# Keys, values and queries of six groups from three fp32r products instead of plain fp32

## The reference

```
q   = layernorm(x) @ Wq.T ;  k, v = ctx @ Wkv.T            # 16 heads of 16, ctx is 192 wide
x   = x + tanh(g0) * softmax(mask(q k' / 4)) v
h   = layernorm(x)
moe = sum over the top 2 of 8 experts: score * (silu(p) * g) @ fc2[e],  p, g = split(h @ fc1[e])
x   = x + tanh(g1) * (moe + (silu(h @ gate_w) * (h @ up_w)) @ down_w)
```

## Time and profile before

| | |
|---|---|
| median of 3 runs | 344.87 us (344.2 to 347.57) |
| the profiled execution | 345.56 us |
| its span in the trace | 343.8 us |
| granted TensorE clock, mean | 0.975 of 2.4 GHz |
| the step loop | from about 22 us to about 155 us |
| PE, DVE, ACT, POOL busy | 90%, 74%, 50%, 35% of the span |

### The profile page before, as it was taken

One profiled execution on the slowest core, in us unless ns is written; L12 is line 12 of the kernel. 1 busy time (PEld: TensorE's weight loads), 2 busy tenths in 40 slices (PEclk: granted clock), 3 DMA queues, 4 the chain that ended last, 5 costly groups with the idle time before them and its releaser, 6 DMA issues.

```text
span 343.8 us, 8094 instructions
## 1 busy us (share of the span) xinstructions
PE 311.0 (90%) x2484; PEld 254.7 (74%) x2484; DVE 253.2 (74%) x780; ACT 170.7 (50%) x325; POOL 119.6 (35%) x133
## 2 busy tenths in 40 slices
PE   8858989989889886777989999999999999999986
PEld 7746767877768764664537488888888988888865
DVE  5566668899989897885889936676666667643795
ACT  2534767766667562555682326544444454424131
POOL 5731121217171715155440062943433433431000
PEclk9998999999999996969999999999999999999999
DMA  8886586666666565211134001333333333202951
GB/s 231 245 235 195 175 214 215 172 185 183 179 187 188 155 187 154 96 65 62 62 110 140 0 15 49 100 96 101 100 109 90 92 95 92 76 27 77 422 176 61
DMA packets 34917, 46.52 MB, mean 135 GB/s; under 512 B 5599, under 2 KB 29539, under 8 KB 34370
## 3 DMA queue, kind: packets, MB, share of 16 engines
q1 hardware_dynamic: 27714, 28.51, 28.9%
q10 hardware_dynamic: 3712, 8.98, 8.1%
q0 software_dynamic: 3456, 8.56, 7.2%
HBM read 21.55 MB, written 12.62 MB: 99 GB/s over the span
## 4 chain that ended last, share of the span: by engine, by line
PE 49%; DVE 19%; SPq 10%; DMA 9%; issue 7%; POOL 4%; ACT 2%; DVEq 0%; POOLq 0%
PE ps L1606 24%; SPq L354 5%; DMA stacks<-work 4%; SPq L361 4%; DVE mx L895 4%; PE ps L1283 3%; DVE x_all L1242 3%; PE ps L1656 2%; PE ps L1348 2%; PE ps L1578 2%; DMA expert_rows<-v_s,slot_u 2%; PE ps L1484 2%; PE ps L1598 2%; POOL dispatched L494 2%; PE ps L1381 2%
## 5 line engine op out<-in xcount | busy, mean ns | idle before, releaser
L539 POOL DMA_INDIRECT expert_rows<-v_s,slot_u x39 | 38.3, 981 | 62.5 <-ACT v_s L804 49.8
L895 DVE TENSOR_REDUCE mx<-ps 128x8 f32<-128x1024 f32 x32 | 39.1, 1223 | 11.5 <-PE ps L1348 10.8
L502 POOL TENSOR_TENSOR work<-work 128x512 bf16<-128x512 f32 x16 | 18.5, 1154 | 60.1 <-ACT work L590 60.0
L621 ACT ACTIVATE probs<-ps 128x1024 f32<-128x1024 f32 x32 | 32.6, 1019 | 11.6 <-PE ps L1381 10.1
L1192 DVE TENSOR_TENSOR act<-ps,sil 128x256 f32<-128x256 f32 x39 | 16.6, 425 | 29.2 <-ACT sil L797 29.1
L797 ACT ACTIVATE sil<-ps 128x256 f32<-128x256 f32 x39 | 15.0, 384 | 39.6 <-PE ps L1606 39.4
L1606 PE MATMUL ps<-fc_hi,xs_hi 128*128 x78 | 34.2, 438 | 0.0
L1606 PE MATMUL ps<-fc_lo,xs_hi 128*128 x78 | 30.9, 396 | 0.0
L1606 PE MATMUL ps<-fc_hi,xs_lo 128*128 x78 | 30.8, 395 | 0.0
L1348 PE MATMUL ps<-stacks 96*128 96x128 bf16 x256 | 20.6, 226 | 10.7 <-DVE mx L895 6.1
L804 ACT ACTIVATE v_s<-ps,wt 128x256 f32<-128x256 f32 x39 | 18.5, 474 | 19.6 <-PE ps L1606 19.6
(11 more groups left out here) (209 smaller groups left out, 808.7 us busy)
## 6 DMA issues: line engine op xcount, KB each, us to landing
stacks<-work SPq DMA_DIRECT2D x93, 128.0 KB, 2.8
xs_in<-dispatched SPq DMA_DIRECT2D x39, 129.0 KB, 2.1
fc_s<-in_fc ACTq DMA_DIRECT2D x8, 512.0 KB, 3.7
fc_s<-in_fc ACTq DMA_DIRECT2D x8, 256.0 KB, 4.3
stacks<-expert_rows SPq DMA_DIRECT2D x2, 1024.0 KB, 5.9
probs<-expert_rows SPq DMA_DIRECT2D x2, 1024.0 KB, 10.0
ctx_s<-in_ctx_t SPq DMA_DIRECT2D x8, 192.0 KB, 3.3
x_all<-in_x SPq DMA_DIRECT2D x1, 1536.0 KB, 7.9
```

The source lines that it names most:

```text
L502: nc.gpsimd.tensor_tensor(out[:, 2, :], rest, out[:, 1, :], ALU.subtract).then_inc(ready, 1)
L539: nc.gpsimd.indirect_dma_start(ys, bass.IndirectOffsetOnAxis(dst_u[:, r:r + 1], 0), y_out[:, r, :], None, bounds_check=2 * T - 1, oob_is_e ...
L621: nc.scalar.activation(probs[:, 2 * j + h], ps_t, ACT.Exp, scale=HD ** -0.5).then_inc(probs_ok[j][h], 1)
L895: nc.vector.reduce_max(mx[:, j, 8 * h:8 * h + 8], ps_s, AX_X).then_inc(max_ok[j][h], 1)
```

## The change

- For groups 2 to 7 `keys`, `queries` and `values_proj` are twelve fp32r matmuls each (`products`) instead of four plain fp32 ones.
- The high half of the context is made by ACT (`ctx_high`), the low one by POOL (`ctx_low`); for the normed tokens ACT writes the high half where it wrote the whole, and DVE makes the low one (`xn_low`).
- The three weights are split once, in step 2: ACT `weight_high`, POOL `weight_low`.
- The high halves lie in the places of the last two experts' weights, so those two are loaded in ACT's last step.
- `load_ctx(s)` moves up in SP's step, from behind `max_rows(s-3, 1)` to ahead of `stack_q(s-2, 0)`.

```diff
@@ SP, loop over s
                 if live(s - 3):
                     max_rows(s - 3, 0)
+                if live(s):
+                    load_ctx(s)
                 if live(s - 2) and s > 2:
                     stack_q(s - 2, 0)
                     stack_q(s - 2, 1)
                     stack_q(s - 2, 2)
                 if live(s - 3):
                     max_rows(s - 3, 1)
-                if live(s):
-                    load_ctx(s)
@@ POOL
+            def weight_low(high_ok, done, low, w, high, ready):
+                pool.wait_ge(high_ok, 1)
+                pool.wait_ge(done, 2)
+                nc.gpsimd.tensor_tensor(low, w, high.bitcast(F32), ALU.subtract).then_inc(ready, 1)
+            def ctx_low(g):
+                pool.wait_ge(ctxh_ok, g - 1)
+                nc.gpsimd.tensor_tensor(ctx_lo[:, g % 2], ctx_s[:, g % 2], ctx_hi[:, g % 2].bitcast(F32),
+                                        ALU.subtract).then_inc(ctxl_ok, 1)
@@ ACT
+                nc.scalar.activation(xn_t[:, :, :] if g < 2 else xn_hi[:, :, :],
+                                     ps_v.rearrange("p (k t) -> p k t", k=2), ACT.Copy).then_inc(xnt_ok, 1)
...
+            def ctx_high(g):
+                sa.wait_ge(ctx_in[g % 2], 16 * (g // 2 + 1))
+                if g >= 4:
+                    sa.wait_ge(k_done, g - 1)
+                    sa.wait_ge(v_done, g - 1)
+                nc.scalar.activation(ctx_hi[:, g % 2], ctx_s[:, g % 2], ACT.Copy).then_inc(ctxh_ok, 1)
@@ ACT, loop over s, behind exp(s - 3, 0, 0) and ahead of norm1(s)
+                if s == 2:
+                    weight_high(wk_in, wk_hi[:, :, :, :], wk_s[:, :, :, :], wkh_ok)
+                    weight_high(wv_in, wv_hi[:, :, :], wv_s[:, :, :], wvh_ok)
+                    ctx_high(2)
+                    weight_high(wq_in, wq_hi[:, :, :, :], wq_s[:, :, :, :], wqh_ok)
+                if live(s) and s > 2:
+                    ctx_high(s)
...
-                if live(s - 2):
+                if live(s - 2) and s - 2 < E - 2:
                     load_experts(s - 2)
+                if s == G + 1:
+                    sa.wait_ge(v_done, G)
+                    sa.wait_ge(q_done, G)
+                    load_experts(E - 2)
+                    load_experts(E - 1)
@@ DVE, loop over s, behind pieces(s - 2, 1)
+                if live(s):
+                    xn_low(s)
@@ DVE
+            def xn_low(g):
+                ve.wait_ge(xnt_ok, g + 1)
+                ve.wait_ge(q_done, g)
+                nc.vector.tensor_tensor(xn_lo[:, :, :], ps_v.rearrange("p (k t) -> p k t", k=2),
+                                        xn_hi[:, :, :].bitcast(F32), ALU.subtract).then_inc(xnl_ok, 1)
@@ PE, keys(g); queries and values_proj in the same way
+                if g >= 2:
+                    pe.wait_ge(ctxl_ok, g - 1)
+                    if g == 2:
+                        pe.wait_ge(wkl_ok, 1)
+                    for c in range(2):
+                        for k in range(2):
+                            last = products(ps_kq[:, TG * c:TG * c + TG], wk_hi[:, k, c, :], wk_lo[:, k, c, :],
+                                            ctx_hi[:, g % 2, k, :], ctx_lo[:, g % 2, k, :], k == 0, k == 1)
+                    last.then_inc(k_done, 1)
+                    return
```

More of the change, by code:

```diff
@@ L212, in build_program @@
         p_f = probs[:, :, :, :].rearrange("p a h t -> p (a h t)")
+        late_1, late_2 = 2 * (E - 2) * 2 * FI, 2 * (E - 2) * D
+        ctx_hi, ctx_lo = over("ctx_hi", "fc1_s", [KC, 2, 2, TG], late_1), over("ctx_lo", "ctx_s", [KC, 2, 2, TG])
+        wk_hi, wk_lo = over("wk_hi", "fc1_s", [KC, 2, 2, P], late_1 + 4 * TG), over("wk_lo", "wk_s", [KC, 2, 2, P])
+        wv_hi, wv_lo = over("wv_hi", "fc1_s", [KC, 2, D], late_1 + 6 * TG), over("wv_lo", "wv_s", [KC, 2, D])
+        wq_hi, wq_lo = over("wq_hi", "fc2_s", [P, 2, 2, P], late_2), over("wq_lo", "wq_s", [P, 2, 2, P])
+        xn_hi = over("xn_hi", "work", [P, 2, TG], 2 * D)
+        xn_lo = over("xn_lo", "fc2_s", [P, 2, TG], late_2 + 2 * TG)
         y_in = [home[:, 8 * D * r:8 * D * (r + 1)].rearrange("p (t k d) -> p t k d", t=CH, k=2)
@@ L260, in build_program @@
             dst_ok ysc0 ysc1 ysc2 ysc3 y_in0 y_in1 y_in2 y_in3 y_half y_added sig_ok out_done
+            wkh_ok wvh_ok wqh_ok wkl_ok wvl_ok wql_ok ctxh_ok ctxl_ok xnl_ok
             fhi_ok flo_ok high_ok low_ok xlo_ok prod_ok hhi_ok f2hi_ok f2lo_ok ahi_ok""".split()
@@ L511, in _ @@
             power1(4, B, 3)
+            def weight_low(high_ok, done, low, w, high, ready):
[6 more added lines that the diff above has]
+                                        ALU.subtract).then_inc(ctxl_ok, 1)
             third(1, kst, k_rest, k_ok[1], k_pc, k_ok[2])
+            weight_low(wkh_ok, k_done, wk_lo[:, :, :, :], wk_s[:, :, :, :], wk_hi[:, :, :, :], wkl_ok)
+            weight_low(wvh_ok, v_done, wv_lo[:, :, :], wv_s[:, :, :], wv_hi[:, :, :], wvl_ok)
+            ctx_low(2)
             third(1, qst, q_rest, q_ok[1], q_pc, q_ok[2])
+            weight_low(wqh_ok, q_done, wq_lo[:, :, :, :], wq_s[:, :, :, :], wq_hi[:, :, :, :], wql_ok)
             for s in range(2, G + 2):
@@ L522, in _ @@
                     third(s, kst, k_rest, k_ok[1], k_pc, k_ok[2])
+                    if live(s + 1):
+                        ctx_low(s + 1)
                     third(s, qst, q_rest, q_ok[1], q_pc, q_ok[2])
@@ L595, in normed_t, with weight_high @@
                     sa.wait_ge(q_done, g)
-                nc.scalar.activation(xn_t[:, :, :], ps_v.rearrange("p (k t) -> p k t", k=2),
-                                     ACT.Copy).then_inc(xnt_ok, 1)
+                nc.scalar.activation(xn_t[:, :, :] if g < 2 else xn_hi[:, :, :],
+                                     ps_v.rearrange("p (k t) -> p k t", k=2), ACT.Copy).then_inc(xnt_ok, 1)
+            def weight_high(loaded, high, w, ready):
+                sa.wait_ge(loaded, 16)
+                nc.scalar.activation(high, w, ACT.Copy).then_inc(ready, 1)
+            def ctx_high(g):
[4 more added lines that the diff above has]
+                nc.scalar.activation(ctx_hi[:, g % 2], ctx_s[:, g % 2], ACT.Copy).then_inc(ctxh_ok, 1)
             def values_in(g):
@@ L1285, in gate_up_1, with products @@
                 last.then_inc(gu_done, 1)
+            def products(out, high, low, x_high, x_low, first, last):
+                for n, (a, b) in enumerate(((high, x_high), (high, x_low), (low, x_high))):
+                    ins = nc.tensor.matmul(out, a, b, start=first and n == 0, stop=last and n == 2)
+                return ins
             def keys(g):
@@ L1307, in queries @@
                 whole = ps_kq if g else ps_q0
+                if g >= 2:
+                    pe.wait_ge(xnl_ok, g - 1)
+                    if g == 2:
+                        pe.wait_ge(wql_ok, 1)
+                    for c in range(2):
+                        for k in range(2):
+                            last = products(whole[:, TG * c:TG * c + TG], wq_hi[:, k, c, :], wq_lo[:, k, c, :],
+                                            xn_hi[:, k, :], xn_lo[:, k, :], k == 0, k == 1)
+                    last.then_inc(q_done, 1)
+                    return
                 for c in range(2):
@@ L1328, in values_proj @@
                 pe.wait_ge(xnt_ok, g + 1)
+                if g >= 2:
+                    pe.wait_ge(xnl_ok, g - 1)
+                    if g == 2:
+                        pe.wait_ge(wvl_ok, 1)
+                    for j in range(2):
+                        rows = slice(P * j, P * j + P)
+                        for k in range(2):
+                            last = products(ps_v[:, D * j:D * j + D], ctx_hi[:, g % 2, k, rows],
+                                            ctx_lo[:, g % 2, k, rows], wv_hi[:, k, :], wv_lo[:, k, :], k == 0, k == 1)
+                    last.then_inc(v_done, 1)
+                    return
                 for j in range(2):
@@ L1601, in _ @@
                         last.then_inc(down_done, 1)
[L1604 to L1607, removed]
             def gate_up(c, j):
```

5 lines of the change are left out of this document (4 added, 1 removed).

## The result

The changed kernel is slower: its time is 1.0225 times that of the kernel before, 95% interval 1.0164 to 1.0286. On the 345.56 us of the profiled execution before, that is 353.3 us (351.2 to 355.4); the working gave 352.3, the forecast 351.6.

A forecast was written before the change was run, and what follows sets the result against it. The prediction took the loop to be bound by SP's DMA queue, the queries' landing and the work behind the first scores. 3.2 + 2.3 + 1.2 = 6.7 on 345.56 gave 352.3, or 351.6 for the median; range 345.5 to 356.5.

The forecast's parts named there:

- the clock falls: Rival: PE waits longer in the loop, its clock drops in two steps, 356 us in all; chance 15%.
- The load in SP's queue, 3.2 us: Context load moved into the gapless part of SP's queue: 0.65 us in each of five steps, 3.2 us slower.
- upper end of 4.7: Upper end for the moved context load: its transfer also delays the queries' landing, another 0.3 us a step.
- the ring: Loop's closed chain: scores release key DMAs, then `max_rows` and query DMAs in SP's queue, then landing; 16.3 us a step.
- `ctx_low` behind T2 to T5, 2.3 us: After first scores start in groups 2 to 5, POOL's subtraction holds DVE's `norm2` or `slot_p`: 0.6 us four times.
- the start, 1.2: Three weight splits at the start: POOL's subtractions hold DVE's first pieces, delaying `max_rows` and query DMAs; 1.2 us slower.
- about 30.5: Sign at the start: `max_rows` of group 0 begins near 30.5 us instead of 29.25.
- The second collision at the start: Upper end for the weight splits: POOL also holds DVE's next `pieces`, 2.4 us instead of 1.2.
- PE's products, nothing: Keys, queries, values on PE: 0.8 us less work a group, 5 in six, becomes waiting; no gain.
- `xn_low`, nothing: New 0.68 us DVE operation, six times, behind `pieces(s-2,1)`: covered by waits, no cost; upper end 1.4 us.
- ACT and the expert loads, nothing: `ctx_high` on half-busy ACT, and the last two experts' loads covered by the last group's attention: no cost.
- the growing wait at T5: Sign for the clock rival: PE's gap before group 5's first scores grows from 1.44 to above 2.5 us.

The follow-up runs named there:

- Experiment 4: Changed kernel with the context load back at its old place and `ctx_high` at the end of ACT's step: 1.0151 times the kernel before.
- experiment 2: Kernel before plus nine unused POOL subtractions where the change has its low halves: 1.0097 times the kernel before, 3.4 us.
- experiment 1: Kernel before with only the context load moved ahead of the query DMAs: 347.73 to 357.07 us against a median of 346.77.
- Experiment 8: Kernel before with `max_rows` issued from ACT's queue instead of SP's: 1.0203 times the kernel before.
- Experiment 5: Changed kernel with POOL's `ctx_low` waiting for the `norm2` of its step: 1.0216 times the kernel before.
- Experiment 3: Changed kernel with each three products replaced by one plain fp32 matmul of the high halves: 1.0283 times the kernel before.
- experiment 9: Kernel before with DVE's update of `dest_f` moved behind the last maximum of the step: 0.9982 times the kernel before.
- experiment 11: Kernel before plus `xn_low` on DVE, result unused, with the values projection waiting for it: 0.9999 times the kernel before.
- Experiment 6: Changed kernel with the weights' high halves and two of POOL's three weight subtractions made earlier: 1.0300 times the kernel before.
- experiment 12: Kernel before plus nine unused ACT copies where the change makes its high halves, load at its old place: 1.0527 times the kernel before.
- the three repairs: Changed kernel with load back and `ctx_high` late, `ctx_low` behind `norm2`, and weights' halves early, all together: 1.0107 times the kernel before.

## Why the prediction was right, point by point

*The time.* 1.0225 on 345.56 is 353.3 against a sum of 352.3. Of the rivals only "the clock falls" (356) is near. Experiment 4 puts the load at 2.6 us (with some 4 to each side) and experiment 2 the work on POOL at 3.4, together 6.0 of the 7.8 us; the sum had 3.2 and 3.5. The other 1.8 lies inside the intervals, and the clock below is the candidate for it. That the sum came within 1 us is in part luck: the share of each step of the loop is not as forecast (below), and the clock, which is in the result, is not in the sum.

*The load in SP's queue, 3.2 us.* The mechanism is in the trace: 0.65 us in the gapless chain (107.33, 108.18, 108.85). The size is not settled: 2.6 by experiment 4, and T1 to T5 longer by 4.1 in the one trace of experiment 1, near the upper end of 4.7 and with two stretches of low clock in it. What does not follow is that SP's queue alone is the ring, the premise with which the prediction opened. Experiment 8 took two issues a step out of that queue, and in its trace T3 to T7 was as before. Whether an issue taken away is not given back, or ACT paid for it instead, or the scatter of single traces hides it, stays open.

*`ctx_low` behind T2 to T5, 2.3 us, and the start, 1.2.* Together they are 3.5, and experiment 2 measured 3.4 (1.8 to 4.9). That POOL's subtractions hold DVE and that this costs time is shown. At the start the rows are the forecast's: two pieces held, `max_rows` at 30.11 against about 30.5. In the loop they are so in part. `norm2` is held behind T2 alone (2.38 us in experiment 2, 2.21 in the changed kernel, 1.42 before) and takes 0.73 in the later steps of all three; what is held behind T3 to T5 are `slot_p` and `slot_u`. Taken together, DVE's operations behind T2 to T5 took 1.8 us more than when free in the kernel before, 2.5 in the changed one and 4.5 in experiment 2. So the 2.3 fits experiment 2, while the changed kernel's own trace holds DVE only 0.7 us longer there: longer behind T2 and T5, shorter behind T3 and T4. (Four times 0.6 is also 2.4, not 2.3.) How the 3.4 divides is not settled. Experiment 5 saw none of `norm2`'s share. The second collision at the start, kept as the upper end (2.4), did happen (33.08), and T0 to T1 is 1.6 to 2.0 us longer in the traces of experiments 3, 4 and 5, which speaks for a start worth more than 1.2. Against it, experiment 2's trace has held pieces and its T0 to T1 is no longer than before, and single traces scatter (14.3 us in experiment 9, 12.8 in 11, both kernels as fast as before). Experiment 6, meant to decide it, did not isolate the start.
The rule used for the start (the Trainium skill, SBUF — State Buffer, Who interferes with whom) is borne out, the cast included (29.37 in experiment 4).

*PE's products, nothing.* 0.12 us apart and 1.5 us a call at full clock, as forecast from the earlier trace rows. Experiment 3 agrees that they do not decide; a gain of some us is not excluded.

*`xn_low`, nothing.* Shown by experiment 11, in the kernel before.

*ACT and the expert loads, nothing.* True as long as the load is early: in the changed kernel `ctx_high` waited once, for 1.1 us. The prediction saw two edits here, one that costs and one that is free; experiment 12 shows that at this place in ACT's queue they are one. The last experts' loads cost nothing: from T7 to the end the traces take the same time (209.4 us in experiment 5, 209.6 before).

*The clock, the step that was missing.* The prediction gave it 15%, as a case by itself; in part it is in the result. The mean granted clock was 0.938 to 0.966 in the four runs, the lowest in the slowest (360.45 us), against 0.975 in the profiled execution before. The mean alone proves little: among eleven executions of the kernel before one had 0.980 and took 343.25 us, another 0.947 and 354.59 us. The places say more. The prediction had put the growing wait at T5, caused by a lighter PE. At T5 it did not grow (1.15 us, 1.44 before); it did at T3 (2.14) and T4 (3.06), and between T1 and T2, and the lighter PE is not needed for it: in experiment 3, with plain fp32 calls on PE, the gap and the low clock between T1 and T2 are there as well, and in experiment 1, with nothing changed but the load, they come at T4 and T5. That late pieces and full transfer engines make the gap is read from the trace, not tested by itself.
The Trainium skill (TensorE: Matmul & The Clock Gate, Why this matters for your kernels) advises against such idle gaps between bursts of matmuls; the trace agrees, with 3.59 us idle and then 0.50.
The length of the gap does not settle it at this place: after 1.63, 1.58 and 1.87 us (experiments 3, 4 and 5) the clock fell, after 1.89 and 2.03 us (experiments 2 and 6) it stayed at 1.00. What decides between them stays open.

*What stays open.* The 1.07% left after the three repairs. In that kernel T1 comes 16.65 us after T0, against 14.7 before, with the second pieces still held by `wq_lo`; T0 to T3 is 2.9 us longer, and no run has taken `wq_lo` away alone, nor edit 6 out of the three repairs.

## What to carry to other kernels

Give each step that is moved two prices: what the queue pays that it is moved into, and what the wait would have cost where the data came too late. Before a compute engine is given an operation that waits for a transfer, ask what stands behind it in its queue: here that was worth about six times what the transfer's issue costs in SP's queue (18 us against 3), and moving the waiting operation to the end of its queue was a third choice. Read the forecast's rows step by step in the trace after, and not the sum alone: here the sum came right, while of the four equal shares behind T2 to T5 the trace showed more holding in two steps and less in the other two. And test both directions, adding to a queue and taking from it, before calling it the bound.

## What the runs showed of the hardware

A DVE cast of 16 columns took 1.19 us under a POOL subtraction of 512 elements, and 0.17 us beside none. An fp32r matmul of 256 columns with its weights started 0.12 us after the one before at 2.4 GHz, and 0.21 us at 1.2 GHz.

A DMA issue on ACT's queue took 0.71 to 1.43 us for the rows of maxima, and ACT's next operation started behind it (31.38 after 29.90 and 1.43). Moved to that queue, the rows landed no sooner (5.96 us in the full stretch, 4.2 before).
The Trainium skill (DMA: Bandwidth & Descriptors, Issuing engines are not separate DMA queues) says that DMAs from several engines share the same transfer engines and save only issue time; experiment 8 agrees, with 5.96 us against 4.2.
